# A first ramp in another order: weight copies, a key-query copy, product 1 and the input statistics are moved in a macaron kernel

## Chip, core and metric

One core of a Trainium2 chip runs the kernel. The metric is device time in microseconds (us), the median of several runs. The engines are PE (TensorE, matmuls), DVE (VectorE), ACT (ScalarE), POOL (GpSimd) and SP (SyncE, which here only issues DMAs). Each works through its own queue in order, and semaphores connect them.

## The reference

x has 4096 rows (2 sequences of 2048) of 256 values. The kernel computes a feed-forward part, a single-head attention over complex projections, and the feed-forward part again:

```python
def fp4_quant_dequant(x):        # blocks of 16 along the last dim
    scale = jnp.maximum(jnp.max(jnp.abs(xb), axis=-1, keepdims=True) / 6.0, 1e-12)
    idx = jnp.searchsorted(_MID, jnp.abs(xb / scale))
    return (_GRID[idx] * jnp.sign(xb) * scale).reshape(shape)
def fp4_linear(x, w):
    return jnp.einsum('bsk,nk->bsn', fp4_quant_dequant(x), fp4_quant_dequant(w))
def _L0_ffn_ref(x, w_gate, w_up, w_down):          # 256 -> 704 -> 256
    h = jax.nn.silu(fp4_linear(x, w_gate)) * fp4_linear(x, w_up)
    return fp4_linear(h, w_down)

x = x + 0.5 * _L0_ffn_ref(_layernorm(x), w_gate, w_up, w_down)
x = x + _L0_attn_ref(_layernorm(x), Wq, bq, Wk, bk, Wv, bv, Wo, bo)
x = x + 0.5 * _L0_ffn_ref(_layernorm(x), w_gate, w_up, w_down)
```

## The kernel before

All of x stays in SBUF as 32 tiles of 128 rows. Products that need float32 accuracy are made of two rounded parts: a value is copied from PSUM to a "hi" tile (ACT), PE subtracts that part from PSUM with a matmul against `neg_ident`, and ACT copies the rest to a "lo" tile. Three matmuls (hi x hi, hi x lo, lo x hi) then replace one.

**A round.** The feed-forward part runs in rounds, `step(c, par)`, c from -2 to 31 on PE (some earlier ones are written out by hand ahead of them). In round c PE makes the gate and up products of tile c+3 in three column parts (`gate_up(.., 0)`, `1`, `2`: 512, 512 and 384 columns, six matmuls each), transposes the quantised hidden values of tile c and the quantised input of tile c+4 (`transpose_chain`, L1650), subtracts the hi part (`chain_lower`, L1800 or L1804), and makes the down product of tile c (`project_down_first` L1772, `project_down_rest` L1779). Tiles -4 to -1 are only the input halves of tiles 0 to 3. DVE makes the block scales of tile c+2 (`scales`, L748 to L760), rounds tile c+1 to the grid (`to_grid`, L772 and L778), scales tile c+2 (`scaled`, L791) and multiplies silu(gate) by up for tile c+3 (`product`, L737). `product(c+3)` frees the gate banks: PE's next `gate_up(.., 0)` waits for it (`gu_read`). ACT takes absolute values (L1310), copies T_hi (`chain_upper`, L1328) and T_lo (`chain_rest`, L1342), makes silu (L1352, waits for part 1 of the gate) and normalises tile c+7 (L1362, waits until the scaled input of the tile before is there, `yx_done`). POOL adds the residual (L510), scales the input part (`scaled_x`, L517, which waits for DVE's rounding of the tile before) and makes zq (L533).

**The first ramp.** Ahead of and inside the first rounds the weights are quantised, transposed and split in nine groups: 0 to 5 of gate and up (`G1` = 6 of them), 6 to 8 of down. A group goes through `transpose_group(n)` on PE, `upper_group(n)` on ACT (hi copy, L1166), `weight_lower(n)` on PE (L1731), `lower_group(n)` on ACT (lo copy, L1171). Groups 0 to 5 share three PSUM banks in turn: `transpose_group(n)` waits for `lower_group(n - 3)`. Beside them the product of key and query weights is made (`m_upper` L1205, `key_query_lower` L1676, `m_lower` L1210; its bank is that of gate part 2), and value times output weights (`value_output_product` L1657, `nv_upper` L1233, `value_output_lower` L1715, `nv_lower` L1239).

**Input statistics.** Tiles 0 to 7 get mean and variance on ACT (`x_means`, `x_variances`, L1189 to L1199), the other 24 on DVE in groups of four (`input_statistics`, L659 to L671): two tiles at the end of one round, two and the summary at the end of the next. `group_std` and `output_std` on POOL make 1/std from them and from the statistics of the new x.

What sets the order is the order of the calls written in each engine's block. The lines of `step` on PE for c = 0, ahead of the change:

```python
gate_up(1 - par, 0)
transpose_group(G1 + 2); pe.wait_ge(wc["lo"], G1 + 2)
transpose_chain(f, c)
weight_lower(G1 + 2)
gate_up(1 - par, 1)
chain_lower(f, c, par)
gate_up(1 - par, 2)
project_down_first(par, dn)
```

## Time and profile before

| | us |
|---|---|
| median of 3 runs | 934.82 (933.93 to 934.95) |
| the profiled execution | 933.85 |
| its span, first to last instruction | 932.0 |
| PE busy | 905.2 |
| DVE busy | 705.0 |
| ACT busy | 651.6 |
| POOL busy | 500.3 |
| DMA, mean of 16 engines | busy in the first slice of 40, hardly after |

The span holds the first feed-forward part with its ramp (to about 274 us), the attention, and the second feed-forward part. The engines' busy times overlap. Behind an instruction of a timeline stands the time for which its engine had been idle just before it and which instruction ended that idleness. Times of instructions are given as start and length; on PE the lengths hold the passage through the array, so that starts are the better measure of pace.

### The profile page before, as it was taken

Reading aid. Unit: us, or ns where it says so; the run is one execution under the profiler, and the core shown is the slowest. Engines: PE = TensorE matmul, PEld = TensorE weight load, DVE = VectorE, ACT = ScalarE, POOL = GpSimd, SP = SyncE. Lnnn points to the kernel's source line nnn. Section 1 sums busy time; section 2 is a strip of 40 time slices with the busy share of each in tenths; the row PEclk is TensorE's granted clock in tenths of the full one; section 3 lists DMA queues with packets and bytes.
Section 4 is the critical chain, followed back from the end, with each engine's and each line's share of the span. In section 5 each row is a group of like instructions: output and inputs, shape, how many; then the busy total and the mean of one; then the engine's idle time right before and its main releaser. Section 6 shows DMA issues by size and latency. Waiting matters only on the chain.

```text
span 932.0 us, 16308 instructions
## 1 busy us (share of the span) xinstructions
PE 905.2 (97%) x5694; PEld 807.7 (87%) x5694; DVE 705.0 (76%) x1164; ACT 651.6 (70%) x1369; POOL 500.3 (54%) x561
## 2 busy tenths in 40 slices
PE   3999999999999999999999999999999999999997
PEld 2788888889888798998998899998988888889896
DVE  7998888998767666655474544545599999999997
ACT  5778887888784575767675576767784678566554
POOL 4556666666530154535663064546577657656562
PEclk9999999999999999999999999999999999999999
DMA  9100000000000000000000000000000000000001
GB/s 317 53 1 1 1 1 2 1 1 1 1 1 1 1 2 1 1 1 2 1 1 1 1 2 1 1 2 1 1 1 1 2 24 24 23 23 24 11 14 46
DMA packets 11953, 13.83 MB, mean 15 GB/s; under 512 B 864, under 2 KB 11104, under 8 KB 11872
## 3 DMA queue, kind: packets, MB, share of 16 engines
q1 hardware_dynamic: 11872, 12.79, 4.1%
q8 instruction: 46, 0.75, 0.3%
q14 instruction: 35, 0.29, 0.1%
HBM read 8.59 MB, written 4.19 MB: 14 GB/s over the span
## 4 chain that ended last, share of the span: by engine, by line
PE 83%; DVE 7%; ACT 4%; POOL 3%; issue 3%; DMA 0%; DVEq 0%; ACTq 0%; POOLq 0%
PE bank L1761 21%; PE bank L2005 19%; PE bank L1650 6%; PE bank_b L1772 6%; PE bank_b L1779 4%; PE bank L2043 4%; PE bank L2047 4%; PE bank L2045 4%; PE bank L1968 2%; PE bank L1800 2%; POOL p_lo L578 1%; PE bank_b L2047 1%; PE bank_b L2043 1%; PE bank_b L2045 1%; PE bank L1986 1%
## 5 line engine op out<-in xcount | busy, mean ns | idle before, releaser
L578 POOL TENSOR_TENSOR p_lo<-s_ring,p_hi 128x512 fp32r<-128x512 f32 x128 | 167.4, 1312 | 219.2 <-ACT p_hi L1509 219.1
L533 POOL TENSOR_TENSOR zq<-grid,s_neg 128x256 f32<-128x256 f32 (+2 forms) x184 | 173.9, 969 | 40.7 <-DVE grid L778 40.7
L940 DVE TENSOR_TENSOR top<-bank,top 128x512 f32<-128x512 f32 x112 | 77.4, 691 | 125.7 <-ACT s_ring L1493 125.7
L1761 PE MATMUL bank<-w_hi,T_hi 128*128 128x512 f32 (+1 forms) x384 | 149.2, 388 | 2.6 <-DVE z L737 1.8
L1761 PE MATMUL bank<-w_hi,T_lo 128*128 128x512 f32 (+1 forms) x384 | 143.9, 375 | 0.0
L1761 PE MATMUL bank<-w_lo,T_hi 128*128 128x512 f32 (+1 forms) x384 | 143.5, 374 | 0.0
L1493 ACT ACTIVATE s_ring<-bank 128x512 f32<-128x512 f32 x128 | 75.9, 593 | 78.1 <-PE bank L2005 78.0
L1328 ACT ACTIVATE T_hi<-bank 128x1024 fp32r<-128x1024 f32 (+1 forms) x68 | 64.6, 950 | 81.5 <-PE bank L1650 81.5
L2043 PE MATMUL bank<-v_hl,p_hi 128*128 128x258 f32 x384 | 109.9, 286 | 0.4 <-DVE x L972 0.2
L2045 PE MATMUL bank<-v_hl,p_hi 128*128 128x256 f32 x384 | 108.2, 282 | 0.0
L2047 PE MATMUL bank<-v_hl,p_lo 128*128 128x258 f32 x384 | 108.2, 282 | 0.0
L2005 PE MATMUL bank<-q_hi,k_hi 128*128 128x512 f32 x256 | 101.3, 396 | 0.8
L2005 PE MATMUL bank<-q_lo,k_hi 128*128 128x512 f32 x256 | 100.7, 393 | 0.0
L2005 PE MATMUL bank<-q_hi,k_lo 128*128 128x512 f32 x256 | 100.3, 392 | 0.0
L1499 ACT ACTIVATE s_ring<-s_ring 128x512 f32<-128x512 f32 x128 | 79.2, 621 | 18.4 <-DVE s_ring L962 18.4
L748 DVE TENSOR_REDUCE amax<-z 128x60 f32<-128x960 f32 (+2 forms) x72 | 74.9, 1040 | 16.6 <-ACT z L1362 13.9
L962 DVE TENSOR_TENSOR s_ring<-s_ring,bank 128x512 f32<-128x512 f32 x128 | 84.9, 678 | 1.3 <-PE bank L1650 0.9
L1509 ACT ACTIVATE p_hi<-s_ring 128x512 fp32r<-128x512 f32 x128 | 80.7, 632 | 7.1 <-PE bank_b L2047 3.5
L1761 PEld LDWEIGHTS bank<-w_hi,T_hi 128*128 128x128 f32 x384 | 72.3, 188 | 12.1 <-issue 3.1
L510 POOL TENSOR_TENSOR x<-x,down 128x256 f32<-128x256 f32 x62 | 46.6, 752 | 64.9 <-ACT down L1317 64.9
L1761 PEld LDWEIGHTS bank<-w_hi,T_lo 128*128 128x128 f32 x384 | 72.1, 188 | 10.6
L1772 PE MATMUL bank_b<-wd_hl,T_hi 128*128 128x256 f32 x600 | 80.5, 280 | 0.0
(228 smaller groups left out, 2281.1 us busy)
## 6 DMA issues: line engine op xcount, KB each, us to landing
out<-x SPq DMA_DIRECT2D x7, 512.0 KB, 2.9
x<-in_L_attn_hidden_states SPq DMA_DIRECT2D x3, 1024.0 KB, 12.3
x<-in_L_attn_hidden_states SPq DMA_DIRECT2D x2, 512.0 KB, 6.9
wraw<-in_L_ffn_w_down SPq DMA_DIRECT2D x1, 704.0 KB, 7.4
wraw<-in_L_ffn_w_up SPq DMA_DIRECT2D x1, 640.0 KB, 4.8
wq_s<-in_L_attn_Wq SPq DMA_DIRECT2D x1, 512.0 KB, 6.4
wk_s<-in_L_attn_Wk SPq DMA_DIRECT2D x1, 512.0 KB, 7.3
wo_s<-in_L_attn_Wo SPq DMA_DIRECT2D x1, 512.0 KB, 8.3
```

Of the source, the lines that this page charges most:

```text
L533: last = nc.gpsimd.tensor_tensor(out=blocks(zq[:, to:to + hi - lo]), in0=blocks(grid[:, lo:hi]), in1=spread(s_neg[:, par, lo // BLOCK:hi / ...
L578: nc.gpsimd.tensor_tensor(out=lower_buf(n, c), in0=score_buf(n, c), in1=upper_buf(n, c).bitcast(F32), op=ALU.subtract).then_inc(plo_done, 1)
L940: nc.vector.tensor_tensor(out=top[:], in0=score_bank(c), in1=other, op=ALU.max).then_inc(top_done, 1)
L962: nc.vector.tensor_tensor(out=p, in0=p, in1=shift_bank, op=ALU.subtract).then_inc(diff_done, 1)
L1499: nc.scalar.activation(p, p, ACT.Exp, scale=SCALE).then_inc(exp_done, 1)
L1509: nc.scalar.activation(upper_buf(n, c), score_buf(n, c), ACT.Copy).then_inc(phi_done, 1)
L1761: last = nc.tensor.matmul(gu[:, lo:hi], lhsT=T[:, par, HK + kd, :], rhs=w[:, kd, lo:hi], start=n == 0, stop=n == len(terms) - 1)
L1772: nc.tensor.matmul(dn, lhsT=T_hi[:, par, k, :], rhs=wd_hl[:, k, half:half + D], start=n == 0, stop=False)
L2005: last = nc.tensor.matmul(score_bank(c), lhsT=kk[:, kd, t], rhs=q[:, kd, :], start=i == 0, stop=i == len(terms) - 1)
L2043: nc.tensor.matmul(o[:, 0:D + 2], lhsT=hi[:, q], rhs=v_hl[:, c, 0:D + 2], start=c == 0, stop=False, skip_group_check=True)
L2045: nc.tensor.matmul(o[:, 0:D], lhsT=hi[:, q], rhs=v_hl[:, c, D + 2:], start=False, stop=False, skip_group_check=True)
L2047: last = nc.tensor.matmul(o[:, 0:D + 2], lhsT=lo[:, q], rhs=v_hl[:, c, 0:D + 2], start=False, stop=c == CH - 1, skip_group_check=True)
```

## The change

Nothing is added to or taken from the arithmetic; instructions change places, all in the first feed-forward part.

- ACT, early ramp: the sums of x tiles 4 to 7 are spread in three pieces (`x_sums`); `upper_group(2)`, `(3)` go ahead of tile -4's absolute values, `upper_group(4)` ahead of `lower_group(2)`; `m_upper` and `m_lower` go behind tile -4's T_lo; `chain_upper(-3)` goes ahead of `normalise(3)`.
- PE, early ramp: `transpose_group(4)` ahead of, `weight_lower(4)` directly behind, `weight_lower(2)` and `(3)`; `key_query_lower` between gate parts 0 and 1 of tile 0; `transpose_chain(-3)` ahead of gate part 2.
- PE, rounds -1 and 0: `weight_lower(6)` and `(7)` move from the end of round -1 behind gate part 0 of round 0, followed at once by gate part 1; `weight_lower(8)` goes behind gate part 2.
- ACT, round 0: `silu_gate(3)` goes ahead of `upper_group(8)` and T_hi.
- DVE, round -2: `scaled(0)` and `product(1)` go ahead of `to_grid(-1)`.
- DVE: the statistics of a group are made one round later (halves after rounds c % 4 = 3 and 0 instead of 2 and 3). POOL: `output_std` one round later; `group_std` is written one round later but at the start of the step, the same place in the queue.

The core of the diff:

```diff
@@ POOL, step
+                    if f == 0 and c >= 0 and c % 4 == 1 and c // 4 + 2 < NT // 4:
+                        group_std(c // 4 + 2)
...
-                    if f == 0 and c >= 0 and c % 4 == 0 and c // 4 + 2 < NT // 4:
-                        group_std(c // 4 + 2)
-                    if f == 0 and c % 4 == 1 and 5 <= c < NT:
-                        output_std((c - 5) // 4)
+                    if f == 0 and c % 4 == 2 and 6 <= c < NT:
+                        output_std((c - 6) // 4)
@@ DVE, blocks_of / input_statistics / step
+                    if f == 0 and c == -2:
+                        scaled(c + 2)
+                        product(c + 3)
+                        to_grid(c + 1)
+                        return
...
-                    g = (c + 10) // 4
-                    if c % 4 == 2 and g < NT // 4:
+                    g = (c + 9) // 4
+                    if c % 4 == 3 and g < NT // 4:
...
-                    if c % 4 == 3 and g < NT // 4:
+                    if c % 4 == 0 and g < NT // 4:
...
-                    if hidden(c + 3):
+                    if hidden(c + 3) and (f or c != -2):
                         product(c + 3)
@@ ACT, step
                     if extra and c == 0:
+                        silu_gate(c + 3)
                         upper_group(G1 + 2)
...
+                    if measured:
+                        minus_mean(c - 2, c - 2)
+                    if c >= (0 if f else 1) and hidden(c + 3):
+                        silu_gate(c + 3)
                     if extra and c == 0:
                         lower_group(G1 + 2)
@@ PE, step
                     if extra and c == 0:
+                        weight_lower(G1)
+                        weight_lower(G1 + 1)
+                        gate_up(1 - par, 1)
                         transpose_group(G1 + 2)
                         pe.wait_ge(wc["lo"], G1 + 2)
...
-                    if extra and c == 0:
-                        weight_lower(G1 + 2)
-                    if gated and c >= 0:
+                    if gated and c >= (0 if f else 1):
                         gate_up(1 - par, 1)
...
                         transpose_group(G1 + 1)
-                        weight_lower(G1)
-                        weight_lower(G1 + 1)
                     if gated and c >= 0:
                         gate_up(1 - par, 2)
+                    if extra and c == 0:
+                        weight_lower(G1 + 2)
@@ PE, ahead of the rounds
             key_query_rest(3)
+            transpose_group(4)
             weight_lower(2)
             weight_lower(3)
-            key_query_lower()
-            transpose_group(4)
+            weight_lower(4)
             transpose_group(5)
             transpose_chain(0, -4)
-            weight_lower(4)
             weight_lower(5)
...
             gate_up(0, 0)
+            key_query_lower()
             gate_up(0, 1)
+            transpose_chain(0, -3)
             pe.wait_ge(aw["m_lo"], 1)
             gate_up(0, 2)
-            transpose_chain(0, -3)
+            chain_lower(0, -3, 1)
             transpose_wo(0)
-            chain_lower(0, -3, 1)
             transpose_wo(1)
```

ACT, early ramp, before, from the absolute values of tile -4 on (w_hi and w_lo are the copies of groups 2 to 5, m_hi and m_lo those of the key-query product):

```order
L1310 ACTIVATE yabs_sb<-y 128x256
L1362 ACTIVATE z<-x,nmr,rstd 128x256
L1166 ACTIVATE w_hi<-bank_b 128x512
L1166 ACTIVATE w_hi<-bank 128x512
L1205 ACTIVATE m_hi<-bank 128x512
L1171 ACTIVATE w_lo<-bank_b 128x512
L1171 ACTIVATE w_lo<-bank 128x512
L1166 ACTIVATE w_hi<-bank 128x384
L1166 ACTIVATE w_hi<-bank_b 128x384
L1328 ACTIVATE T_hi<-bank 128x256
```

The same stretch with the change, from the copy of group 2 on:

```order
L1171 ACTIVATE w_hi<-bank_b 128x512
L1171 ACTIVATE w_hi<-bank 128x512
L1318 ACTIVATE yabs_sb<-y 128x256
L1370 ACTIVATE z<-x,nmr,rstd 128x256
L1171 ACTIVATE w_hi<-bank 128x384
L1176 ACTIVATE w_lo<-bank_b 128x512
L1176 ACTIVATE w_lo<-bank 128x512
L1171 ACTIVATE w_hi<-bank_b 128x384
L1336 ACTIVATE T_hi<-bank 128x256
```

The hi copies of groups 2 and 3 stand ahead of the absolute values, that of group 4 ahead of the lo copies, and m_hi is no longer among them.

PE, round 0, before: from the transposes of group 8 and of tile 0 (zq) to chain_lower (L1800), with gate part 1 between:

```order
L1650 MATMUL bank_b<-ident,wst 128x128 x2
L1650 MATMUL bank<-ident,zq 128x128 x8
L1731 MATMUL bank_b<-wd_hl,neg_ident 128x512
L1761 MATMUL bank<-w_hi,T_hi 128x512
L1761 MATMUL bank<-w_lo,T_hi 128x512
L1761 MATMUL bank<-w_hi,T_lo 128x512
L1761 MATMUL bank<-w_hi,T_hi 128x512
L1761 MATMUL bank<-w_lo,T_hi 128x512
L1761 MATMUL bank<-w_hi,T_lo 128x512
L1800 MATMUL bank<-T_hi,neg_ident 128x512 x2
```

The same place with the change (L1813 is chain_lower, L1744 weight_lower(8), L1785 the down product):

```order
L1663 MATMUL bank_b<-ident,wst 128x128 x2
L1663 MATMUL bank<-ident,zq 128x128 x8
L1813 MATMUL bank<-T_hi,neg_ident 128x512 x2
L1774 MATMUL bank<-w_hi,T_hi 128x384
L1774 MATMUL bank<-w_lo,T_hi 128x384
L1774 MATMUL bank<-w_hi,T_lo 128x384
L1774 MATMUL bank<-w_hi,T_hi 128x384
L1774 MATMUL bank<-w_lo,T_hi 128x384
L1774 MATMUL bank<-w_hi,T_lo 128x384
L1744 MATMUL bank_b<-wd_hl,neg_ident 128x512
L1785 MATMUL bank_b<-wd_hl,T_hi 128x256 x10
```

Gate part 1 has left the place between the transposes and chain_lower, and weight_lower(8) stands directly ahead of the down product.

ACT, rounds -1 and 0, before, from `lower_group(6)` on (wd_hl are the copies of the down groups):

```order
L1171 ACTIVATE wd_hl<-bank_b 128x2x256
L1171 ACTIVATE wd_hl<-bank 128x2x256
L1362 ACTIVATE z<-x,nmr,rstd 128x256
L1310 ACTIVATE bank<-y 128x960
L1166 ACTIVATE wd_hl<-bank_b 128x2x256
L1328 ACTIVATE T_hi<-bank 128x1024
L1171 ACTIVATE wd_hl<-bank_b 128x2x256
L1352 ACTIVATE silu<-bank 128x704
```

With the change:

```order
L1176 ACTIVATE wd_hl<-bank_b 128x2x256
L1176 ACTIVATE wd_hl<-bank 128x2x256
L1370 ACTIVATE z<-x,nmr,rstd 128x256
L1318 ACTIVATE bank<-y 128x960
L1360 ACTIVATE silu<-bank 128x704
L1171 ACTIVATE wd_hl<-bank_b 128x2x256
L1336 ACTIVATE T_hi<-bank 128x1024
L1176 ACTIVATE wd_hl<-bank_b 128x2x256
```

The silu of tile 3 stands ahead of T_hi of tile 0 instead of behind it.

## Rows read from the trace of the kernel before

**Rows 1.** The page, part 2: granted TensorE clock, tenths, 40 slices of the span.

```profile
PEclk9999999999999999999999999999999999999999
```

**Rows 2.** PE in order of time: start, length, line, tiles, shape, count [idle before <-releaser].

```profile
12.11 3.75 PE L1657 MATMUL bank<-wk_s,wq_s 128*128 128x256 f32 x8 [12.11 <-DMA wk_s<-in_L_attn_Wk]
...
22.94 0.50 PE L1731 MATMUL bank_b<-w_hi,neg_ident 128*128 128x512 f32 x1 [2.01 <-ACT w_hi L1166]
...
27.12 0.47 PE L1761 MATMUL bank<-w_hi,T_hi 128*128 128x512 f32 x1 [0.75 <-ACT T_lo L1342]
...
37.40 0.44 PE L1650 MATMUL bank<-ident,zq 128*128 128x128 f32 x2 [0.32 <-POOL zq L533]
...
41.55 1.89 PE L1657 MATMUL bank_b<-woT,wv_s 128*128 128x256 f32 x8
...
44.12 0.50 PE L1715 MATMUL bank_b<-nv,neg_ident 128*128 128x512 f32 x1
...
50.62 0.51 PE L1731 MATMUL bank<-wd_hl,neg_ident 128*128 128x512 f32 x1 [0.36 <-ACT wd_hl L1166]
50.97 0.40 PE L1761 MATMUL bank<-w_hi,T_hi 128*128 128x512 f32 x1
...
52.80 1.04 PE L1650 MATMUL bank<-ident,zq 128*128 128x128 f32 x8
...
55.42 0.63 PE L1800 MATMUL bank<-T_hi,neg_ident 128*128 128x512 f32 x2
...
56.93 1.34 PE L1772 MATMUL bank_b<-wd_hl,T_hi 128*128 128x256 f32 x10
...
58.93 0.40 PE L1761 MATMUL bank<-w_hi,T_hi 128*128 128x512 f32 x1
...
73.24 0.40 PE L1761 MATMUL bank<-w_hi,T_hi 128*128 128x512 f32 x1
...
80.79 0.47 PE L1761 MATMUL bank<-w_hi,T_hi 128*128 128x512 f32 x1 [0.24 <-DVE z L737]
...
197.08 0.47 PE L1761 MATMUL bank<-w_hi,T_hi 128*128 128x512 f32 x1 [0.23 <-DVE z L737]
```

**Rows 3.** ACT in order of time, same columns.

```profile
22.32 0.57 ACT L1166 ACTIVATE w_hi<-bank_b 128x512 fp32r<-128x512 f32 x1
...
30.15 0.76 ACT L1352 ACTIVATE silu<-bank 128x704 f32<-128x704 f32 x1
...
42.03 0.59 ACT L1362 ACTIVATE z<-x,nmr,rstd 128x256 f32<-128x256 f32 x1
...
43.47 0.60 ACT L1233 ACTIVATE nv<-bank_b 128x512 fp32r<-128x512 f32 x1
...
49.60 0.38 ACT L1342 ACTIVATE T_lo<-bank 128x256 fp32r<-128x256 f32 x1
...
50.47 0.59 ACT L1171 ACTIVATE wd_hl<-bank_b 128x512 fp32r<-128x512 f32 x1
...
51.66 0.59 ACT L1362 ACTIVATE z<-x,nmr,rstd 128x256 f32<-128x256 f32 x1
...
53.87 1.03 ACT L1328 ACTIVATE T_hi<-bank 128x1024 fp32r<-128x1024 f32 x1 [0.24 <-PE bank L1650]
```

**Rows 4.** DVE in order of time, same columns.

```profile
39.95 0.36 DVE L772 SCALAR_TENSOR_TENSOR rounded<-yabs_sb,y 128x256 f32<-128x256 f32 x1
...
50.29 0.74 DVE L659 BATCH_NORM_STATS2 stats<-x 128x6 f32<-128x256 f32 x2
...
51.56 0.17 DVE L671 TENSOR_SCALAR var<-mv 128x4 f32<-128x4 f32 x1
52.28 1.15 DVE L748 TENSOR_REDUCE amax<-z 128x60 f32<-128x960 f32 x1 [0.56 <-ACT z L1362]
...
57.30 0.89 DVE L737 TENSOR_TENSOR z<-bank,silu 128x704 f32<-128x704 f32 x1
```

**Rows 5.** POOL in order of time, same columns: scaled_x of tile 0.

```profile
40.46 0.79 POOL L517 TENSOR_TENSOR y<-z,s_inv 128x256 f32<-128x256 f32 x1 [3.11 <-DVE rounded L772]
```

More of the change, by code:

```diff
@@ L1180, in weight_abs, with x_sums, minus_means @@
                                      scale=ROUND).then_inc(wc["abs"], 1)
-            def x_means(g):
-                q = slice(4 * g, 4 * g + 4)
-                act.wait_ge(x_in_s[g], 16)
-                if g:
-                    act.wait_ge(x_var, 4 * g)
-                for t in range(4 * g, 4 * g + 4):
+            def x_sums(first, last):
+                act.wait_ge(x_in_s[first // 4], 16)
+                if first >= 4:
+                    act.wait_ge(x_var, 4)
+                for t in range(first, last):
                     nc.scalar.activation(xjunk[:, t % 4, :], x[:, t, :], ACT.Identity,
                                          accum_out=total[:, t:t + 1]).then_inc(x_tot, 1)
+            def minus_means(g):
+                q = slice(4 * g, 4 * g + 4)
                 act.wait_ge(x_tot, 4 * (g + 1))
@@ L1193, in x_means, with x_variances @@
                 nc.scalar.activation(nmean_s[:, q], total[:, q], ACT.Copy, scale=-1.0 / D / ROOT).then_inc(x_nm, 1)
-            def x_variances(g):
-                act.wait_ge(x_nm, g + 1)
-                for t in range(4 * g, 4 * g + 4):
+            def x_variances(first, last):
+                act.wait_ge(x_nm, first // 4 + 1)
+                for t in range(first, last):
                     nc.scalar.activation(xjunk[:, t % 4, :], x[:, t, :], ACT.Square, scale=1.0 / ROOT,
@@ L1450, in _ @@
             absolute(-3)
+            m_upper()
+            normalise(2)
+            x_sums(7, 8)
             m_lower()
-            normalise(2)
-            x_means(1)
+            minus_means(1)
             silu_gate(0)
-            normalise(3)
-            absolute(-2)
             chain_upper(-3, 1)
@@ L1459, in _ @@
             chain_rest(-3, 1)
-            x_variances(1)
+            normalise(3)
+            absolute(-2)
+            x_variances(4, 8)
             weight_abs(5)
```

18 lines of the change are left out of this document (8 added, 10 removed).

## The prediction

> **What bounds the kernel now.** I read the busy times of the page first: PE (TensorE) works 905.2 of the span's 932.0 us (the table above), and its granted clock is full in all 40 slices [rows 1]. A kernel of this kind gains only where PE stands still, and loses where it is made to. So I went through PE in order of time, noting each idle time and what ended it [rows 2], and laid beside it what ACT (ScalarE), DVE (VectorE) and POOL (GpSimd) did at those moments [rows 3 to 5]. After the first DMA, PE idles in the ramp 2.01 us at 22.94, 0.75 at 27.12, 0.32 at 37.40 and 0.36 at 50.62. From 50.97 on it is in the regular rounds: 58.93 to 73.24 is two rounds, 7.16 each. Every fourth round one is longer: 73.24 to 80.79 is 7.55, with 0.24 of idle that DVE's product ends; the pattern comes five times, first at 80.79 and last at 197.08. So the sum is PE's start of round 1 (58.93) with the change, plus what happens to the five long rounds.
>
> Overlap matters in the sums: on ACT an instruction lets the next one start about 0.1 before its own end, so a 128x512 copy (0.57 to 0.60 long, [rows 3]) moves ACT on by 0.48, a 128x384 one by 0.38, the silu (0.76) by 0.65. From the end of a copy to a matmul that waits for it pass 0.05 to 0.15.
>
> **Part 1, the first gate product.** Before, ACT goes from 22.32 through ten copies to T_lo of tile -4, for which the gate at 27.12 waits [rows 2, 3]. The change takes three 128x512 copies out of that stretch: two of groups 2 and 3 go where ACT was idle before 21.5, m_hi behind T_lo. That is 3 x 0.48 = 1.44. In their place comes a wait: group 5 can be transposed only when lower_group(2), now second in the stretch, has freed bank_b (22.70 + 0.60 = 23.30), and PE's three transposes with their latency end at about 23.95, 0.25 after ACT is free for upper_group(5). Net 1.2: the gate starts at 25.9. key_query_lower now stands inside the gate products (one 128x512 matmul, 0.35), so the silu of tile 0 starts at 29.3, not 30.15: the gain is now 0.85. The x sums moved into ACT's idle time cost nothing there, and their result is not used until the means.
>
> **Part 2, tile -2.** The wait of 0.32 at 37.40 is for zq, behind group_std(1) on POOL, behind the variances on ACT. Between silu and the last variance ACT has the same instructions in another order, so that chain moves by the same 0.85, to 36.55. PE is ready for it at 35.7 and waits 0.85 instead of 0.32. The gain stays 0.85.
>
> **Part 3, product 1 ahead of tile -1's grid.** DVE, some 1.1 earlier by then because it no longer waits for weight_abs(4), reaches the end of the scales of tile 0 at 38.85 (39.95 before, [rows 4]). Now scaled(0) and product(1), each some 0.9 (the product at 57.30 takes 0.89), come first, and the rounding of tile -1 starts at 40.6, after 39.95 before. Nobody needs product 1 so early: PE asks for it only behind value_output_lower, which starts at 44.12 [rows 2]. But POOL's scaled_x(0) waits for that rounding: 41.1 to 41.7, where it was 40.46 to 41.25 [rows 5]; ACT's normalise(5) waits for that, then absolute(0), then nv_upper. Before, nv_upper started at 43.47, 1.44 behind normalise(5) at 42.03 [rows 3], and value_output_lower followed at 44.12. Now: 41.75 + 1.44 = 43.2, ends 43.8, PE at 43.85. PE is ready at 43.27 and waits 0.55. The gain falls from 0.85 to 0.3. Bounds: no wait at all (gain 0.85) if DVE is 0.6 earlier than I have it; no gain if it is 0.3 later. I take 0.3.
>
> **Part 4, round 0.** This is the largest term. Before [rows 2, 3], the two weight_lower of w_down groups 6 and 7 stood at the end of the step ahead (idle 0.36 at 50.62), gate part 1 (1.40) stood between tile 0's transposes (52.80) and chain_lower (55.42), and weight_lower(8) had all of part 1 and 2 behind it before the down product (56.93) needed it. Now: the step starts when T_lo of tile -1 is there: 49.60 + 0.38 - 0.3 + 0.15 = 49.85. Gate part 0 (1.39) goes first, so the first weight_lower starts at 51.25 and ends at 51.75. ACT, idle until then, runs lower_group(6) and (7) (2 x 0.48) from 51.8, where it ran them from 50.47. Then come normalise(6) at 52.75 (51.66 before), absolute and upper_group(8) (before, 51.66 to 53.87 less some 0.3 of idle: 1.9), and in their midst now the silu (0.65): T_hi of tile 0 starts at 55.3 and ends at 56.35. PE meanwhile does gate part 0, the two weight_lower (0.6), part 1 (1.39), the group's transposes (0.44) and tile 0's (0.88): 49.85 + 4.7 = 54.55. Then it waits for T_hi until 56.4: **1.85 us**, where part 1 used to cover the copy. After chain_lower and part 2 (1.51, from 55.42 to 56.93) weight_lower(8) starts at 57.9 and ends at 58.4; the down product waits for ACT's lower_group(8) (0.60) until 59.2, PE being ready at 58.3: **0.9 us**. The down product takes 2.0 (56.93 to 58.93), so round 1 starts at 61.2.
>
> DVE in this round arrives at the same time [rows 4]: amax from 53.4 (52.28 before, after normalise(6)), 5.02 to the end of y (52.28 to 57.30), then the second half of the statistics of group 2, which before ran a round earlier (50.29 to 51.7: 1.4, or up to 1.8 if the small nmean instruction waits for POOL's zq), then the product (0.89) and 0.15 to PE: 60.85 to 61.25. So this is no further term, but it closes the way to a smaller loss: even with ACT faster, PE could not start before about 60.9.
>
> **Sum of the ramp:** 61.2 - 58.93 = 2.3 us later. From then on PE has the same instructions, and DVE is back ahead of it a round later (no statistics in rounds 1 and 2).
>
> **Part 5, the statistics one round later.** Each group's two halves still stand in two neighbouring rounds, the heavy half ahead of the product. The long round moves from the fourth to the fifth and so on; with groups 3 to 7 there are five, as before, 0.4 each (7.55 against 7.16). On POOL group_std keeps its place in the queue; output_std comes a round later, where its readers are rounds away. I take 0. Bounds: -2.0 if all five go, +2.0 if each doubles; nothing in the rows speaks for either end, since the work in a round and its limits are the same. At the end of the first feed-forward part output_std leaves the residual of tile 29 free, but PE waits there for other copies: 0.
>
> The profiled execution took 933.85 us (span 932.0); with +2.3 it is 936.15. The median of the runs shown is 934.82, 0.97 above it, so the forecast is **937.1 us**, 0.25% slower. About 0.2% (1.9 us) is what a measurement can tell from no change here.
>
> **One rule against the change.** PE's first product, after 12.11 us of idleness, ran 3.75 us for eight halves, while the same form later took 1.89 [rows 2], though the granted clock is noted as full there too [rows 1]; after the idle 2.01 at 22.94 the gates ran at their full pace of 0.23 each. The longest new wait (1.85) is shorter than that one, so no term. The Trainium skill ("TensorE: Matmul & The Clock Gate", Part 1) says that an array that has been idle is gated to 1.2 GHz and only activity releases it: by that rule a new wait can cost beyond its length.
>
> **The rivals.**
> - *The ramp's gain stays, the loss of round 0 is smaller.* If nv_upper is not late (part 3, 0.85 kept) and statistics take their short form, round 1 starts between 60.3 and 60.65 (all of part 4 shifted by 0.55) and the loss is 1.4 to 1.7: 936.2 to 936.5. For it: my times for DVE around 39 rest on sums of several small steps. Against it: both the T_hi and the DVE chain lie behind the late lower_group(6). Within 0.2%. Chance 0.20.
> - *The long rounds go.* If with the shifted halves DVE's heavy round falls where it has slack, 2.0 come back: 937.1 - 2.0 = 935.1. Against it: the slack of each round is the same before. Chance 0.06.
> - *Faster.* Round 0's copies are hidden after all: the place is chain_lower(0), the price 1.85 + 0.9 and the shift 0.85 kept. It decides at ACT's T_hi: were it done by 54.5 (as before, at 54.9), PE would go straight through, keep 0.85 and the 0.36 of 50.62, and end at 934.82 - 1.2 = 933.6. It would need lower_group(6) not to wait for PE, which the order forbids. Chance 0.05, of which 0.03 by over 0.2% (with the long rounds gone too).
> - *The clock falls.* After a wait of 1.85 the matmuls run at half pace for about as long as the first product shows (3.75 against 1.89): +1.9, 939.0. Chance 0.03.
> The forecast has 0.66.
>
> **How the numbers follow.** Own range of the forecast: loss 1.9 to 3.0, so 936.7 to 937.8. The range to be given holds the first rival too and the noise between runs (933.93 to 934.95, half a microsecond each way): 935.5 to 938.2; outside lie the faster case, some of the long-round case and the clock. Slower: 0.66 + 0.03 = 0.69; same: 0.20 + 0.06 + 0.02 = 0.28; faster 0.03.
>
> **What would show it.** In the profile after: the first gate at 25.9; PE waiting for zq at 36.5 (0.85) and for nv_hi before value_output_lower (0.55); ACT's lower_group(6) at about 51.8 and PE idle some 1.85 before chain_lower(0), released by T_hi, and 0.9 before the first down matmul, released by the w_down copy; round 1 starting at 61.2; long rounds ending a round later, five of them. I am wrong if chain_lower(0) does not wait, or if the count or size of the long rounds changes.

## The result and the profile after

The changed kernel takes 936.55 us in the median (936.33 to 939.2, 8 runs), the kernel before 934.91 beside it (933.93 to 936.41, 8 runs). The ratio of their comparable executions is 1.0023, with a 95% interval of 1.0014 to 1.0032: slower by 0.23%, against a forecast of 937.1 us and 0.25%. (The ratio isn't that of the two medians, which stand only 1.64 us, 0.18%, apart; why medians say less here is told under The experiments.) The profiled execution took 936.33 us with a span of 934.5 (before 933.85 and 932.0), so 2.48 us more where the sum of the prediction said 2.3. Nearly all of it lies in the first feed-forward part: 2.32 at the start of round 1, 2.43 at its last down product (271.52 against 269.09), 0.1 more later.

PE in order of time, in the changed kernel: all instructions of the first ramp that it stood idle ahead of (but the first one), and the starts of round 0, of `weight_lower(8)`, of round 1 and of the first long round. Columns as in rows 2.

```profile
22.89 0.44 PE L1744 MATMUL bank<-w_hi,neg_ident 128*128 128x384 f32 x1 [0.97 <-ACT w_hi L1171]
...
24.56 0.45 PE L1744 MATMUL bank_b<-w_hi,neg_ident 128*128 128x384 f32 x1 [0.36 <-ACT w_hi L1171]
...
25.97 0.47 PE L1774 MATMUL bank<-w_hi,T_hi 128*128 128x512 f32 x1 [0.75 <-ACT T_lo L1350]
...
36.55 0.44 PE L1663 MATMUL bank<-ident,zq 128*128 128x128 f32 x2 [0.91 <-POOL zq L533]
...
43.96 0.50 PE L1728 MATMUL bank_b<-nv,neg_ident 128*128 128x512 f32 x1 [0.62 <-ACT nv L1241]
...
49.88 0.50 PE L1774 MATMUL bank<-w_hi,T_hi 128*128 128x512 f32 x1
...
56.38 0.73 PE L1813 MATMUL bank<-T_hi,neg_ident 128*128 128x512 f32 x2 [1.68 <-ACT T_hi L1336]
...
57.98 0.39 PE L1744 MATMUL bank_b<-wd_hl,neg_ident 128*128 128x512 f32 x1
59.06 1.45 PE L1785 MATMUL bank_b<-wd_hl,T_hi 128*128 128x256 f32 x10 [0.69 <-ACT wd_hl L1176]
...
61.25 0.47 PE L1774 MATMUL bank<-w_hi,T_hi 128*128 128x512 f32 x1
...
90.32 0.47 PE L1774 MATMUL bank<-w_hi,T_hi 128*128 128x512 f32 x1 [0.23 <-DVE z L737]
```

The reader is to see two things. The ramp is ahead of the kernel before at 25.97 (27.12 in rows 2) and at 36.55 (37.40), and behind it at 61.25 (58.93): the loss is made in round 0, at 56.38 and 59.06. And the long rounds are still there, the first now at 90.32, five of them with 0.23 of idle each, as in rows 2.

ACT over the same round 0 (columns as in rows 3). The copy at 51.81 is the late `lower_group(6)`, for which it waited 1.39; T_hi of tile 0 follows at 55.28, where rows 3 had it at 53.87.

```profile
51.81 0.60 ACT L1176 ACTIVATE wd_hl<-bank_b 128x512 fp32r<-128x512 f32 x1 [1.39 <-PE bank_b L1744]
52.30 0.59 ACT L1176 ACTIVATE wd_hl<-bank 128x512 fp32r<-128x512 f32 x1
52.78 0.60 ACT L1370 ACTIVATE z<-x,nmr,rstd 128x256 f32<-128x256 f32 x1
53.27 0.97 ACT L1318 ACTIVATE bank<-y 128x960 f32<-128x960 f32 x1
54.17 0.75 ACT L1360 ACTIVATE silu<-bank 128x704 f32<-128x704 f32 x1
54.80 0.60 ACT L1171 ACTIVATE wd_hl<-bank_b 128x512 fp32r<-128x512 f32 x1
55.28 1.04 ACT L1336 ACTIVATE T_hi<-bank 128x1024 fp32r<-128x1024 f32 x1
58.41 0.60 ACT L1176 ACTIVATE wd_hl<-bank_b 128x512 fp32r<-128x512 f32 x1 [2.09 <-PE bank_b L1744]
```

And DVE: its `product(2)` ahead of the round, which waits for PE, and at the end of the round the second half of the statistics of group 2, then `product(3)`, which ends at 61.11. PE's last five down matmuls start at 60.58, some 0.12 apart, so by my estimate PE would be free at about 61.17, and gate part 0 starts at 61.25. The two arrive together.

```profile
48.40 0.89 DVE L737 TENSOR_TENSOR z<-bank,silu 128x704 f32<-128x704 f32 x1 [0.62 <-PE bank L1774]
...
58.42 0.75 DVE L659 BATCH_NORM_STATS2 stats<-x 128x6 f32<-128x256 f32 x2
59.21 0.38 DVE L667 BATCH_NORM_AGGREGATE mv<-stats 128x2 f32<-128x6 f32 x4
59.63 0.62 DVE L669 TENSOR_SCALAR nmean<-mv 128x4 f32<-128x4 f32 x1
...
60.23 0.88 DVE L737 TENSOR_TENSOR z<-bank,silu 128x704 f32<-128x704 f32 x1
```

### The profile page after: what moved, and what is told of

Same layout as the page of the kernel before. It is cut to its first block, busy times and chain, and to the rows that moved or that the text cites. A ratio compares the mean times of both kernels' runs of the same rounds, so it can differ in the third digit from the quotient of the medians.

```text
span 934.5 us, 16310 instructions
## 1 busy us (share of the span) xinstructions
PE 905.1 (97%) x5694; PEld 807.5 (86%) x5694; DVE 705.0 (75%) x1164; ACT 652.1 (70%) x1369; POOL 499.1 (53%) x561
## 4 chain that ended last, share of the span: by engine, by line
PE 81%; DVE 8%; ACT 4%; issue 3%; POOL 3%; DMA 0%; DVEq 0%; ACTq 0%; POOLq 0%
PE bank L1774 21%; PE bank L2019 19%; PE bank L1663 6%; PE bank_b L1785 6%; PE bank_b L1792 4%; PE bank L2057 4%; PE bank L2061 4%; PE bank L2059 4%; PE bank L1982 2%; PE bank L1813 2%; POOL p_lo L578 2%; PE bank_b L2061 1%; PE bank_b L2057 1%; PE bank_b L2059 1%; PE bank L2000 1%
## 5 line engine op out<-in xcount | busy, mean ns | idle before, releaser
L1785 PE MATMUL bank_b<-wd_hl,T_hi 128*128 128x256 f32 x600 | 80.5, 280 | 0.7 <-ACT wd_hl L1176 0.7
```

The source lines that it names most:

```text
L1785: nc.tensor.matmul(dn, lhsT=T_hi[:, par, k, :], rhs=wd_hl[:, k, half:half + D], start=n == 0, stop=False)
```

## The experiments

**How their times are compared.** The times of one kernel fall into three groups, and the mean granted clock of the execution names the group, with few exceptions. Of 81 executions of the kernel before, 41 had 1.000 (median 934.02 us), 26 had 0.998 (935.02) and 14 had 0.996 (936.27). What happens in the latter is shown below, at the experiment with the added products. A median over all executions depends on how many of each it holds, so beside the medians I compare the 1.000 groups where a kernel has one, else the 0.998 groups. How far to trust that: the kernel before ran beside each of three sets of experiments and had 934.01, 933.95 and 934.11 at 1.000, so differences between kernels of different sets are uncertain by 0.1 to 0.2. Some groups hold two executions. And two executions lie some 1 us above the others of their group, 936.64 in "round 0 undone" (the others 935.23 to 935.51) and 934.26 in "early ramp only" (933.04 to 933.35).

| kernel | median, all | ratio (95%) | at clock 1.000 (n) | at 0.998 (n) |
|---|---|---|---|---|
| before | | | 934.02 (41) | 935.02 (26) |
| changed | 936.55 | 1.0023 (1.0014 to 1.0032) | 936.41 (6) | 937.77 (1) |
| round 0 undone | 936.63 | 1.0014 (1.0005 to 1.0023) | 935.34 (5) | 936.75 (5) |
| order of round 0 only | 938.01 | 1.0039 (1.0027 to 1.0052) | none | 937.99 (4) |
| statistics only | 936.44 | 1.0024 (1.0014 to 1.0033) | 935.57 (2) | 936.29 (5) |
| round 0 and statistics undone | 935.47 | 1.0004 (0.9996 to 1.0013) | 933.93 (5) | 935.51 (5) |
| early ramp only | 933.35 | 0.9993 (0.9984 to 1.0001) | 933.28 (7) | 934.70 (3) |
| early ramp, zq first | 933.81 | 0.9999 (0.9988 to 1.001) | 933.44 (6) | 934.61 (2) |
| silu back | 936.82 | 1.0026 (1.0017 to 1.0035) | 936.73 (6) | 938.00 (2) |
| summary late | 931.76 | 0.9979 (0.9971 to 0.9988) | 931.57 (6) | 932.91 (2) |
| early ramp and summary late | 930.99 | 0.9964 (0.9953 to 0.9976) | 930.93 (3) | 932.15 (2) |
| the same, 34 products added | 931.2 | 0.997 (0.9959 to 0.9981) | 930.81 (3) | 931.70 (2) |
| before, 34 products added | 935.01 | 1.0001 (0.9992 to 1.0009) | 934.01 (4) | 935.12 (6) |
| before, 60 products added | 936.42 | 1.0021 (1.0012 to 1.0029) | 936.42 (11) | none |

**Round 0 undone.** The changed kernel; the lines of PE's and ACT's step for c = 0 go back to their old places.

```diff
@@ ACT, step
                     if extra and c == 0:
-                        silu_gate(c + 3)
                         upper_group(G1 + 2)
...
+                    if extra and c == 0:
+                        lower_group(G1 + 2)
                     if measured:
                         minus_mean(c - 2, c - 2)
@@ PE, step
                     if extra and c == 0:
-                        weight_lower(G1)
-                        weight_lower(G1 + 1)
-                        gate_up(1 - par, 1)
                         transpose_group(G1 + 2)
...
+                    if extra and c == 0:
+                        weight_lower(G1 + 2)
+                    if gated and c >= 0:
                         gate_up(1 - par, 1)
...
                         transpose_group(G1 + 1)
+                        weight_lower(G1)
+                        weight_lower(G1 + 1)
```

> The changed kernel with PE's and ACT's order of round 0 put back as it was before (weight_lower(6) and (7) at the end of round -1, gate part 1 between tile 0's transposes and chain_lower, weight_lower(8) ahead of gate part 1, silu_gate(3) behind T_hi). All else stays changed, the statistics too. Theory A (the two waits of round 0 are the loss, but DVE, with the second half of the statistics of group 2 now in round 0, reaches its product late as well): the T_hi wait of 1.68 and the wd_hl wait of 0.69 in round 0 vanish, PE waits instead for DVE's product ahead of round 1, which starts at about 60.0 (59.5 to 60.3; before 58.93, changed kernel about 61.2): +0.6 to +1.3 us against the kernel before. Theory B (the order of round 0 is the whole loss and the statistics cost nothing there): round 1 at 58.6, -0.3 us. Theory C (the statistics or product 1 are the loss, the order innocent): as the changed kernel, +2.3 us.

Measured: 935.34 at clock 1.000, +1.32 against before, just above the upper end of theory A. Both waits of round 0 are gone; the only wait from 52.2 on is the one at the start of round 1, for DVE's product (PE, in order of time):

```profile
52.16 0.50 PE L1743 MATMUL bank<-wd_hl,neg_ident 128*128 128x512 f32 x1 [0.36 <-ACT wd_hl L1171]
...
61.67 0.47 PE L1773 MATMUL bank<-w_hi,T_hi 128*128 128x512 f32 x1 [1.04 <-DVE z L737]
```

(This profiled execution is of the 0.998 group: PE's wait for zq, at 36.55 in the changed kernel, ends at 38.25 here, 1.70 late, which is why its 61.67 is later than the 61.25 of the changed kernel. The idle times can be compared, the absolute times can't; distances from that wait can.) So the order of round 0 is not the whole loss: without it the statistics keep more than half.

**Order of round 0 only.** The kernel before, with the same lines moved the other way (the mirror image of the diff above).

> The kernel before with nothing but the new order of round 0 on PE and ACT. Theory A: the waits for T_hi and for the w_down copy come as in the changed kernel (1.7 and 0.7 there), round 1 starts at about 61.5 (58.93 before), +2.6 us (2.3 to 2.9); a little more than the whole change since the early ramp's gain is missing. Theory C (the order is innocent, the loss comes from the statistics or product 1): 0. The long rounds stay at 80.79 + 2.6 and so on, five of them.

Measured: no execution at 1.000; at 0.998 it is 937.99 against 935.02, +2.97. The sign and the mechanism of theory A hold; the size is at the upper end of its range or a little above (with only the 0.998 group to go by, it is uncertain by some 0.3, and by the trace it is 2.85: from the end of the wait for zq, 38.50, to round 1, 62.88, pass 24.38 us, before 21.53). PE's waits in round 0:

```profile
51.62 0.47 PE L1762 MATMUL bank<-w_hi,T_hi 128*128 128x512 f32 x1 [0.60 <-DVE z L737]
...
58.09 0.73 PE L1801 MATMUL bank<-T_hi,neg_ident 128*128 128x512 f32 x2 [1.69 <-ACT T_hi L1328]
...
60.77 1.44 PE L1773 MATMUL bank_b<-wd_hl,T_hi 128*128 128x256 f32 x10 [0.69 <-ACT wd_hl L1171]
```

The last two are those of the changed kernel to 0.01. The first one is new: gate part 0 of round 0 needs the banks that `product(2)` frees, and before, the two `weight_lower` stood ahead of it and covered that time. In the changed kernel they are gone from there too, but its `product(2)` ends at 49.29, before PE asks at 49.88. Most of that is the early ramp's doing. In the early-ramp-only kernel, below, `product(2)` ends 0.14 after PE starts `weight_lower(6)` (and so it does in early ramp and summary late); in the kernel before it ends 0.60 after it (50.37 against 49.77). With product 1 ahead of the grid too, in the kernel with round 0 and statistics undone, it has to wait for PE and ends 0.32 ahead of it:

```profile
49.37 0.89 DVE L737 TENSOR_TENSOR z<-bank,silu 128x704 f32<-128x704 f32 x1
50.12 0.50 PE L1738 MATMUL bank_b<-wd_hl,neg_ident 128*128 128x512 f32 x1
```

```profile
49.87 0.89 DVE L737 TENSOR_TENSOR z<-bank,silu 128x704 f32<-128x704 f32 x1 [0.60 <-PE bank L1773]
```

So this order alone is dearer (2.85 to 2.97) than the whole change (2.39).

**Statistics only.** The kernel before with the statistics one round later.

```diff
@@ POOL, step: group_std(c // 4 + 2) at c % 4 == 1, output_std((c - 6) // 4) at c % 4 == 2
@@ DVE, input_statistics
-                    g = (c + 10) // 4
-                    if c % 4 == 2 and g < NT // 4:
+                    g = (c + 9) // 4
+                    if c % 4 == 3 and g < NT // 4:
...
-                    if c % 4 == 3 and g < NT // 4:
+                    if c % 4 == 0 and g < NT // 4:
```

> The kernel before with only the statistics, group_std and output_std one round later. Theory A: DVE reaches product(3) in round 0 late, PE idles 0.8 to 1.4 ahead of round 1 (starts 59.7 to 60.3), the five long rounds stay 0.4 each and come one round later: +0.8 to +1.4 us. Theory B (DVE has room for the second half in round 0, the trace of the changed kernel shows no wait for the product there): 0. A gain, with the long rounds gone: -2.0.

Measured: +1.27 at 0.998, theory A (+1.55 from the two executions at 1.000, a little above it; by the trace +1.19 from the wait for zq to round 1). PE's wait for the product at the start of round 1 is 1.05:

```profile
62.38 0.47 PE L1761 MATMUL bank<-w_hi,T_hi 128*128 128x512 f32 x1 [1.05 <-DVE z L737]
```

The next wait for that product is 29.1 later (91.49, 0.23), four rounds on: the long rounds stay, each a round later. The loss lies in round 0 alone, because the second half of group 2 has moved into it, and there DVE has no slack.

**Round 0 and statistics undone.** The changed kernel with both undone; the early ramp and product 1 ahead of the grid remain.

> The changed kernel with both undone, the order of round 0 and the later statistics; what stays is the new early ramp and product 1 ahead of tile -1's grid. Theory A: the early ramp gains 0.85 and the wait for nv_hi (0.62 in the changed kernel) takes 0.55 of it back: round 1 starts at 58.6, -0.3 us (-0.5 to 0). Theory D (product 1 ahead costs nothing): -0.85 us or more. Theory E (the early gain is lost again before round 1 whatever follows): 0.

Measured: 933.93 at 1.000, -0.09 against before (in theory A's range, at its upper end; its value of -0.3 is 0.2 too good). The wait for nv_hi is there with 0.63.

**Early ramp only.** The same, and in DVE's round -2 the old order:

```diff
-                    if f == 0 and c == -2:
-                        scaled(c + 2)
-                        product(c + 3)
-                        to_grid(c + 1)
-                        return
```

> The kernel before with the new early ramp alone (weight copies, key-query copy, x sums, chain of tile -3); product 1 stands behind tile -1's grid again, round 0 and the statistics as before. Compared at the same granted clock (before: 934.0 us at 1.000). Theory A: the wait for nv_hi (0.63 with product 1 ahead) is gone, the gain of 0.85 reaches round 1 (58.1 to 58.3, before 58.93): -0.65 to -0.9 us. Theory E (what the early ramp gains is lost anyway behind POOL's zq or at nv_hi): -0.1 us, as with product 1 ahead.

Measured: 933.28 at 1.000, -0.74 (theory A). The wait for nv_hi is gone, and product 1 ahead of the grid costs 933.93 - 933.28 = +0.65 in this place (0.59 when each is compared with the kernel before that ran beside it). The profiled execution is the slow one of its group, 934.26: its first product started at 13.45, its first gate at 27.18 and its round 1 at 59.27. The new early ramp seems to feel when the data come: with the first product at 12.36, 12.88 and 13.45 (early ramp and summary late, zq first, this one) the first gate is at 26.09, 26.41 and 27.18. The old one, with 2.01 of idle to spare ahead of 22.94, had its gate at 27.12 with the first product at 12.11 and at 27.11 with 12.67 (summary late).

**zq first.** The early ramp alone, and on POOL

```diff
-            group_std(1)
             first_ffn(-3, 1)
+            group_std(1)
```

> The early ramp alone, and on POOL the zq of tile -2 ahead of group_std(1), for which PE idled 0.91 at 36.55 in the changed kernel. Theory F (PE's wait for zq is the limit of the early ramp): the wait goes and round 1 starts another 0.8 us sooner, -1.6 us against the kernel before. Theory G (DVE and POOL set the pace behind it): the wait for zq shrinks, but the same time comes back at nv_hi ahead of value_output_lower, so that it is worth 0 to 0.2 us over the early ramp alone.

Measured: 933.44 at 1.000, 0.16 more than the early ramp alone. The wait of 0.9 for zq is gone and has come back whole:

```profile
43.72 0.50 PE L1722 MATMUL bank_b<-nv,neg_ident 128*128 128x512 f32 x1 [0.87 <-ACT nv L1236]
```

Theory G. PE is not the bound of the stretch from 36 to 44; DVE, POOL and ACT are, on the way to nv_hi.

**Silu back.** The changed kernel with `silu_gate(3)` of round 0 behind T_hi and `lower_group(8)`.

```diff
@@ ACT, step
                     if extra and c == 0:
-                        silu_gate(c + 3)
                         upper_group(G1 + 2)
...
-                    if c >= (0 if f else 1) and hidden(c + 3):
+                    if c >= 0 and hidden(c + 3):
                         silu_gate(c + 3)
```

> The changed kernel with only silu_gate(3) of round 0 put back behind T_hi and lower_group(8) on ACT. T_hi then starts 0.65 sooner and PE's wait of 1.68 ahead of chain_lower(0) shrinks to about 1.0. Theory A (DVE's product, late through the statistics, stands right behind that wait): the gain is lost again ahead of round 1, which starts at 61.2 as before, or later, since the product now waits for silu as well: 0 to +0.3 us against the changed kernel (936.4 at clock 1.000). Theory H (the T_hi wait alone sets the start of round 1): -0.65, 935.8.

Measured: 936.73 at 1.000, +0.32 against the changed kernel, theory A. Part of the 0.32 need not be the order: in this trace PE is 0.39 late already at its wait for zq (36.94), and from there to round 1 pass 24.69 us, in the changed kernel 24.70. The T_hi wait shrinks and the rest moves on to the product:

```profile
56.20 0.73 PE L1812 MATMUL bank<-T_hi,neg_ident 128*128 128x512 f32 x2 [1.11 <-ACT T_hi L1336]
...
61.63 0.47 PE L1773 MATMUL bank<-w_hi,T_hi 128*128 128x512 f32 x1 [0.48 <-DVE z L737]
```

This shows that DVE's chain stands right behind ACT's in round 0, as the prediction had it: with T_hi sooner, PE waits for the product instead.

**Summary late.** The kernel before; in the second round of each group the two mean-and-variance instructions and the two small ones behind the product.

```diff
@@ DVE, input_statistics (second half)
-                        group_statistics(g)
+                        if c < 0:
+                            group_statistics(g)
@@ DVE, step, behind product(c + 3)
+                    if f == 0 and c >= 0 and c % 4 == 3 and (c + 10) // 4 < NT // 4:
+                        group_statistics((c + 10) // 4)
```

> The kernel before with the summary of a statistics group (two means-and-variances instructions and two small ones, some 1.4 us behind the halves) on DVE behind the product of the round instead of ahead of it; the halves stay. It tests what makes the long rounds (7.55 against 7.16, five of them). If they come from all of the statistics that stand ahead of the product in the second round, moving the summary removes them: -2.0 us (5 x 0.40), at granted clock 1.000 932.0 us, and no wait for the product at 80.79. If the next round then waits in its turn, since DVE has the same work in two rounds: 0.

Measured: 931.57 at 1.000, -2.45 (expected -2.0). All five waits are gone. Round 3 on PE is 80.35 - 73.20 = 7.15 (7.55 in rows 2), and the next one 7.15 too (in the kernel before it ran from 80.79 to 88.00, 7.21):

```profile
73.20 0.40 PE L1764 MATMUL bank<-w_hi,T_hi 128*128 128x512 f32 x1
...
80.35 0.40 PE L1764 MATMUL bank<-w_hi,T_hi 128*128 128x512 f32 x1
...
87.50 0.40 PE L1764 MATMUL bank<-w_hi,T_hi 128*128 128x512 f32 x1
```

So a long round cost 0.46, not 0.40: 5 x 0.46 = 2.3 of the 2.45. DVE in that round:

```profile
77.91 0.75 DVE L659 BATCH_NORM_STATS2 stats<-x 128x6 f32<-128x256 f32 x2
78.62 0.89 DVE L737 TENSOR_TENSOR z<-bank,silu 128x704 f32<-128x704 f32 x1
79.43 0.37 DVE L667 BATCH_NORM_AGGREGATE mv<-stats 128x2 f32<-128x6 f32 x4
79.83 0.17 DVE L669 TENSOR_SCALAR nmean<-mv 128x4 f32<-128x4 f32 x1
...
86.16 0.89 DVE L737 TENSOR_TENSOR z<-bank,silu 128x704 f32<-128x704 f32 x1 [1.14 <-PE bank L1764]
```

The product of the next round still waits 1.14 for PE: the slack to take the summary was in that next round all along, and the five long rounds were a matter of order within DVE's queue.

**Early ramp and summary late.** The two gains in one kernel.

> The new early ramp alone (without product 1 ahead, the order of round 0 and the later statistics) together with the summary of the statistics behind the product. Compared at granted clock 1.000: if the two gains, 0.7 and 2.4 us, lie at places that don't touch, they add: 934.0 - 3.1 = 930.9 us. If the early ramp's gain is lost to DVE as soon as the long rounds are gone: 931.6, as the late summary alone.

Measured: 930.93 at 1.000, -3.09: they add. With a median of 930.99 and a ratio of 0.9964 (0.9953 to 0.9976) this is faster than both kernels, by 0.36% of the kernel before.

**60 products added.** The kernel before, with work put in PE's first idle time:

```diff
             def key_query_product():
+                for _ in range(60):
+                    nc.tensor.matmul(m_bank[:, 0:P], lhsT=ident[:], rhs=ident[:], start=True, stop=True,
+                                     skip_group_check=True)
                 pe.wait_ge(qk_in, 16 * 2)
```

> The kernel before with 60 products of ident by ident (128 columns each, into the bank that the key-query product overwrites) put ahead of the first product, where PE is idle for 12.1 us; that is work added which no result needs. It tests where the half-pace stretches between 23.5 and 31.5 come from that some executions of every kernel show (granted clock 0.50 for 3.3 us or, in others, 6.7 us, at a cost of 1.05 to 1.2 us each; of 26 executions of the kernel before, 13 had none, 9 one, 4 two). Theory W (they follow from how little PE did before): the first product takes 1.9 us instead of 3.75, no execution has such a stretch, and the median falls from 934.5 to 934.0 or a little below. Theory V (it is the pauses at 21 to 27 that bring them, whatever was before): the first product takes 1.9 us, but as many executions as before have the stretch, median 934.5. Theory U (the added products run late into the ramp): slower, up to 936.

First, what the 0.998 and 0.996 groups are. The stretches of the statistics-only kernel, whose profiled execution is of the 0.996 group (columns: stretch, its length, busy time of PE, PEld, DVE, ACT, POOL, granted clock, DMA share, GB/s):

```profile
24.00:26.00 2.00, 2.00 (x10) 1.81 (x10) 2.00 (x2) 1.74 (x4) 1.02 (x2) 0.60 1.10 348
26.00:28.00 2.00, 1.26 (x4) 0.85 (x4) 1.02 (x4) 1.97 (x7) 0.00 (x0) 0.50 0.41 128
28.00:30.00 2.00, 2.00 (x5) 1.55 (x6) 1.85 (x7) 2.00 (x9) 0.62 (x1) 0.50 0.01 4
30.00:32.00 2.00, 2.00 (x8) 1.58 (x7) 1.22 (x2) 0.79 (x5) 0.70 (x1) 0.69 0.01 4
```

PE's granted clock stood at 0.50, its lower level of 1.2 GHz, from 24.4 to 31.2 there (0.60 in the first row is 1.6 us of the lower level, 0.69 in the last 1.2 us). In the round-0-undone kernel, of the 0.998 group, the rows of 26 to 28 and 28 to 30 have 0.60 and 0.54, so the lower level from 26.4 to 29.8, and PE's matmuls of 128x512 start 0.43 apart instead of 0.23:

```profile
26.83 0.63 PE L1773 MATMUL bank<-w_hi,T_lo 128*128 128x512 f32 x1
27.26 0.63 PE L1773 MATMUL bank<-w_hi,T_hi 128*128 128x512 f32 x1
...
30.06 0.39 PE L1773 MATMUL bank<-w_hi,T_hi 128*128 128x512 f32 x1
30.29 0.40 PE L1773 MATMUL bank<-w_lo,T_hi 128*128 128x512 f32 x1
```

Ahead of the stretch PE had pauses of 1.77 us at 22.93 in the first kernel and of 1.09, 0.36 and 0.75 at 23.02, 24.70 and 26.11 in the second; the kernel before has such pauses too (rows 2) and stays at 1.00 in its trace. Measured with the 60 products: all 11 executions at clock 1.000, where of the kernel before one in two is not. That part of theory W came out. But the median is 936.42: the 60 took 15.18 us and ran until 17.6, past the arrival of the data, which is theory U. That explains 1.9 of the 2.4 us (first gate at 29.00 against 27.12, and still 1.9 behind at 724.10); in the profiled execution some 0.7 more come in the second feed-forward part, after a wait of 0.57 for DVE at 787.89 that the kernel before doesn't have. Why, no run shows.

```profile
2.56 15.18 PE L1664 MATMUL bank<-ident 128*128 128x128 f32 x120 [2.56 <-ACT neg_ident L1159]
...
17.57 1.89 PE L1657 MATMUL bank<-wk_s,wq_s 128*128 128x256 f32 x8
```

**34 products added**, to the kernel before and to the fastest one (early ramp and summary late): the same edit with `range(34)`.

> The kernel before with the same 34 products in PE's first idle time. Theory W: all executions at clock 1.000, median 934.0. Theory V: half of them with a half-pace stretch, median 934.5. Against the 60 of the other experiment (936.4, since they ran until 17.6, 5 us past the arrival of the data), the 34 should cost nothing.

> The same, and 34 products of ident by ident (work that no result needs) in PE's first idle time: at the 0.253 us apiece that 60 of them took, from 2.56 to 11.2, ahead of the data of the key-query product at 12.1. Theory W (how little PE did before brings the half-pace stretches): no execution has one, and the median is that of the executions at clock 1.000, 930.9. Theory V: as many as without have one, median some 0.6 higher. The first product, 1.9 us instead of 3.75, might also let the wait ahead of the lo parts of the weights at 22.9 begin sooner, but that wait ends with ACT, so no further gain: 930.9; at most 1.9 less (929.0) if the chain to ACT's copies ran over PE.

Measured: the 34 ran a little longer than expected, until 13.2 and 12.3, but the added work costs nothing (934.01 against 934.02, and 930.81 against 930.93, at 1.000), the first product takes 1.89 and 1.99, and yet 7 of 11 and 4 of 7 executions have the lower clock, about as many as of the kernel before beside them (13 of 22). So theory W falls in the form in which I put it: work ahead of the first product doesn't keep the clock up. What the 60 did besides was to fill most of PE's pauses until 24 (1.08 at 24.82 and 0.75 at 29.00 remained). Busy time of PE from 12 to 24, first with 60, then with 34 added to the kernel before (two stretches of 6 us each):

```profile
12.00:18.00 6.00, 6.00 (x54) 5.95 (x53) 5.62 (x7) 3.80 (x13) 4.82 (x6) 1.00 1.06 370
18.00:24.00 6.00, 5.75 (x33) 4.41 (x31) 2.35 (x8) 3.17 (x7) 2.56 (x2) 1.00 1.10 350
```

```profile
12.00:18.00 6.00, 4.86 (x32) 4.03 (x31) 5.63 (x7) 4.74 (x16) 4.66 (x6) 1.00 1.06 373
18.00:24.00 6.00, 3.85 (x18) 2.10 (x17) 5.24 (x14) 4.24 (x10) 3.71 (x6) 1.00 1.10 349
```

11.75 of 12 us busy against 8.71. That this is the cause is argued, not shown: the 60 also moved the whole ramp 1.9 us back, and no kernel was run that fills the pauses without doing so, or that does so without filling them.

## Why the prediction was right, and where not

**The sum.** At clock 1.000 the whole change costs 936.41 - 934.02 = 2.39 us; forecast 2.3. Taken off one after the other, the parts are:

| part | forecast | measured | by the traces | from |
|---|---|---|---|---|
| early ramp | -0.85 | -0.74 | -0.85 | early ramp only - before |
| product 1 ahead of the grid | +0.55 | +0.65 | +0.67 | round 0 and statistics undone - early ramp only |
| statistics in round 0 | no term: hidden behind the order | +1.41 | +1.24 | round 0 undone - round 0 and statistics undone |
| order of round 0 | +2.6 (61.2 against 58.6) | +1.07 on top | +1.28 on top | changed - round 0 undone |

The traces give the split a second time, free of the clock, whose half-pace stretches all end before 32. The early ramp is the end of PE's wait for zq, 36.55 in the changed kernel and 37.40 before. The rest is the way from there to the start of round 1: 21.53 us before, 21.51 with the early ramp only, 22.18 with product 1 ahead, 23.42 with round 0 undone, 24.70 in the changed kernel. The two ways agree within 0.2.

The forecast put the last two on one line: ACT's chain sets the start of round 1, DVE arrives with it. Together they measured 2.48 (forecast 2.6). Alone, the statistics cost 1.19 to 1.55 and the order 2.85 to 2.97, so they overlap, which is what "closes the way to a smaller loss" meant.

**Part 1** (right): first gate at 25.97 (25.9), silu at 29.23 (29.3). Its list of PE's idle times leaves out two small ones, 0.20 at 16.51 and 0.17 at 32.02; neither changes the sum. **Part 2** (right): the wait for zq at 36.55 is 0.91 (0.85). **Part 3** (right): rounding of tile -1 at 40.49 (40.6), nv_hi at 43.33 (43.2), PE at 43.96 after 0.62 (43.85, 0.55). The rival in which nv_upper is not late, with 0.20 the largest, didn't come.

**Part 4** (right, with two terms a little off): step at 49.88 (49.85), `lower_group(6)` at 51.81 (51.8), T_hi at 55.28 (55.3), PE released at 56.38 (56.4). Its wait is 1.68, not 1.85, since PE was ready at 54.70, not 54.55; the down product waits 0.69, not 0.9. Round 1 starts at 61.25 (61.2). What the prediction missed is a side effect: with the two `weight_lower` gone from the end of round -1, PE would have waited 0.60 for `product(2)`, as the order-only kernel shows. The early ramp takes most of that away (0.60 becomes 0.14) and product 1 ahead of the grid the rest (the 0.62 of the DVE row at 48.40 above, where DVE waits for PE). The forecast named no wait there and was right for the changed kernel, but gave no reason, and that was luck. It counted the moved product as pure loss (+0.55); but for that last 0.14 it is one.

**Part 5** (right): five long rounds, 0.23 of idle each, one round later; hardly a change after round 1 (2.32 behind there, 2.43 at the end of the first feed-forward part). The size of a long round was off: 0.46 with what it does to the next, not 0.40. And the reason given against "the long rounds go", that DVE's slack in each round is the same before, was too quick. They do go for a change of order within DVE's queue, only not for this one.

**The level.** The step that failed is the last one: adding 0.97 because the profiled execution was that much under the median of three. That gap is not a constant. It is the difference between an execution at clock 1.000 and one at 0.998 (934.02 and 935.02); by their times two of those three runs were of the latter kind, while 6 of the 8 of the changed kernel had 1.000. Without the 0.97 the forecast would have been 936.15, and 936.41 was measured at 1.000. The median of 936.55 lies between that and the 937.1, below the forecast's own range (936.7 to 937.8) and just above the 936.2 to 936.5 of the first rival. It was the traces, not the time, that told the two apart: nv_upper was late and the statistics took their long form (the nmean of 0.62).

**The clock as a rival.** It was put at the wrong place, and on the evidence of one trace: that the gates behind the 2.01 of idle ran at full pace holds for that execution, not for every other. Behind the new wait of 1.68 the granted clock stays at 1.00:

```profile
54.00:56.00 2.00, 0.69 (x7) 0.46 (x5) 1.97 (x5) 2.00 (x4) 0.00 (x0) 1.00 0.00 0
56.00:58.00 2.00, 1.62 (x9) 1.54 (x9) 1.97 (x3) 0.32 (x1) 0.95 (x2) 1.00 0.01 4
```

Where it does fall is the early ramp, between 24 and 31, in kernels with and without the change. There the Trainium skill's rule ("TensorE: Matmul & The Clock Gate", Part 1), that the array runs at half rate until activity releases it, agrees with the trace as far as the two levels go. What the traces add is that the level fell after no long idleness: from 22 to 24 PE was busy 1.07 of 2 us in the statistics-only kernel and 0.85 in the round-0-undone one. What decides in which execution it happens, no run here shows.

## What to carry to other kernels

A copy that waits for PE must not be queued ahead of the copy that PE waits for next: here two `weight_lower` moved behind 1.39 us of gate product held up ACT's copies and everything behind them, which is 1.68 us of idle on PE; the third `weight_lower`, put directly ahead of the product that needs its copy, made 0.69 more. Before moving work to a later round, look at whether that round has slack at its last handover; work that only has to be done some time belongs behind the instruction that frees a buffer (the summary behind the product: -2.45 us), not ahead of it. And before two medians are subtracted, sort the executions by their mean granted clock.

## What the runs showed of the hardware

- **A half-pace stretch in one execution of two.** With nothing changed, 40 of 81 executions of the kernel before had a mean granted clock under 1.000, and cost 1.00 or 2.25 us more. The traces of such executions, all of other kernels, show granted clock 0.50 in the early ramp for some 3.4 us or twice as long (26.4 to 29.8 and 24.4 to 31.2 above), which fits the means of 0.998 and 0.996. Whether it costs more with the new early ramp is open: the 0.998 groups lie 0.7 to 1.3 us above the 1.000 groups in the kernels with the old one, 0.9 to 1.6 in those with the new one, mostly from few executions.
- **The granted clock doesn't show the start.** The first product, after 12 us of idleness, takes 3.75 us with the clock noted as 1.00; with added products ahead of it, about half, 1.89, also at 1.00. Its slowness costs nothing here (934.01 against 934.02).
- **A tiny DVE instruction takes 0.62 or 0.17 us.** `nmean`, on 128x4, took 0.62 in all rounds where it ran ahead of the product beside POOL's zq, and 0.17 at 79.83 behind the product (where POOL's last zq still ran until 79.97). The Trainium skill ("SBUF — State Buffer", "SBUF: two separate sides") says that DVE, in some of its modes or with two inputs in SBUF, and POOL share a pair of ports that one holds for a whole instruction while the other waits; the 0.62 would agree with that, but no run here separates it from other causes.
